# Four scores together, and VectorE's bias on the last two heads, in two attention stages of a transformer on one Trainium2 core

## The reference, cut to what matters

```python
# first attention (L0_attn)
scores = jnp.einsum('bhqd,bhkd->bhqk', q * scale, k)
scores = scores + position_bias * 8.0      # bucket of the distance, constant beyond 64
attn = jax.nn.softmax(scores, axis=-1)
ctx_out = jnp.einsum('bhqk,bhkd->bhqd', attn, v)
# rotary attention (in L2_ffn)
q = q * cos + _rotate_half(q) * sin
k = k * cos + _rotate_half(k) * sin
attn = jax.nn.softmax(jnp.einsum('bhqd,bhkd->bhqk', q, k) / sqrt(HD), axis=-1)
ao = jnp.einsum('bhqk,bhkd->bhqd', attn, v)
```

## Time and profile before

| | |
|---|---|
| time, median of 3 runs | 5949.95 us (5943.79 to 5955.69) |
| time of the profiled execution | 5956.9 us |
| its span | 5955.1 us |
| mean granted TensorE clock | 0.949 |
| busy: PE, PEld, DVE, ACT, POOL | 93%, 47%, 68%, 46%, 18% |
| first attention, first to last score | 81 to 969 us |
| rotary attention, first to last score | 2597 to 3348 us |

### The profile page before, as it was taken

How to read it: one execution, slowest core, us unless ns; L and a number is a source line. 1 busy time by engine, 2 the same in 40 slices (tenths; PEclk the granted TensorE clock), 3 DMA queues, 4 the chain that set the end, 5 groups by cost and what they waited for, 6 DMA issues and landing times. The chain is left out here.

```text
span 5955.1 us, 87145 instructions
## 1 busy us (share of the span) xinstructions
PE 5515.6 (93%) x32386; PEld 2785.2 (47%) x32386; DVE 4035.8 (68%) x7079; ACT 2747.2 (46%) x4392; POOL 1089.8 (18%) x731
## 2 busy tenths in 40 slices
PE   6999997789999999999999899979999999997999
PEld 2333333445477777742222377633333433434676
DVE  7888885775677777779989422367777777773412
ACT  4656665222233333357777534334444344442333
POOL 0110100220022232310120000023433333341000
PEclk7999998788999999999999899989999999998999
DMA  4211210001211111111111100000000000001000
GB/s 87 45 31 29 40 20 11 0 0 33 41 29 27 27 32 21 36 21 32 36 36 25 30 1 1 1 23 14 13 12 12 12 12 12 12 15 36 4 4 8
DMA packets 119335, 131.32 MB, mean 22 GB/s; under 512 B 44772, under 2 KB 68116, under 8 KB 118596
## 3 DMA queue, kind: packets, MB, share of 16 engines
q1 hardware_dynamic: 118408, 125.07, 10.1%
q10 hardware_dynamic: 504, 0.69, 0.1%
HBM read 102.29 MB, written 22.07 MB: 21 GB/s over the span
## 5 line engine op out<-in xcount | busy, mean ns | idle before, releaser
L3540 DVE TENSOR_REDUCE wide_max_parts<-wide_p 128x2 f32<-128x1024 f32 x512 | 613.8, 1219 | 133.2 <-PE wide_p L3444 120.8
L732 ACT ACTIVATE attn_w<-l_p 128x512 f32<-128x512 f32 x1024 | 549.3, 597 | 276.1 <-DVE l_p L1176 152.0
L2488 PE MATMUL caus_p<-caus_x_one,big 128*128 128x129 f32 x4608 | 639.8, 286 | 0.0
L583 DVE TENSOR_REDUCE l_max_parts<-l_p 128x2 f32<-128x1024 f32 x512 | 601.8, 1218 | 47.5 <-PE l_p L559 43.1
L2572 ACT ACTIVATE big<-caus_p 128x512 f32<-128x512 f32 (+3 forms) x768 | 345.5, 489 | 573.2 <-PE caus_p L2474 417.7
L583 DVE TENSOR_REDUCE rot_max_parts<-rot_p 128x2 f32<-128x1024 f32 x488 | 574.0, 1218 | 49.8 <-PE rot_p L559 47.5
L2488 PEld LDWEIGHTS caus_p<-caus_x_one,big 128*128 128x128 f32 x4608 | 590.2, 198 | 35.6 <-issue 2.2
L2932 ACT ACTIVATE moe_hidden<-moe_experts,moe_b 128x512 f32<-128x512 f32 x512 | 351.0, 687 | 527.0 <-PE moe_experts L2920 526.9
L3463 PE MATMUL wide_p<-wide_q,wide_k 64*128 64x512 f32 x2048 | 529.2, 595 | 0.0
L3643 ACT ACTIVATE attn_w<-wide_p 128x1024 f32<-128x1024 f32 x342 | 350.1, 1024 | 354.6 <-PE wide_p L3463 351.0
L2942 PEld LDWEIGHTS moe_experts<-big,moe_hidden 128*128 128x128 f32 x4096 | 474.2, 192 | 50.4 <-issue 49.3
(11 more groups left out here) (552 smaller groups left out, 8250.7 us busy)
## 6 DMA issues: line engine op xcount, KB each, us to landing
pair_q_stack<-q_parts SPq DMA_DIRECT2D x576, 32.0 KB
pair_k_stack<-k_parts SPq DMA_DIRECT2D x576, 32.0 KB
wide_inverse<-inverse_rows SPq DMA_DIRECT2D x64, 256.0 KB
l_q_stack<-q_parts SPq DMA_DIRECT2D x279, 32.0 KB
l_k_stack<-k_parts SPq DMA_DIRECT2D x279, 32.0 KB
big<-in_L_ffn_W SPq DMA_DIRECT2D x32, 256.0 KB, 5.9
q_parts<-pair_parts_q SPq DMA_DIRECT2D x8, 768.0 KB, 3.6
k_parts<-pair_parts_k SPq DMA_DIRECT2D x8, 768.0 KB, 3.6
```

The costliest lines, as they stand in the source:

```text
L583: self.nc.vector.tensor_reduce(self.max_parts[:, 2 * p:2 * p + 2, n, half], pair[:, :, 0:self.width(n, half)], AX.X, ALU.max).then_inc(*se ...
L732: self.nc.scalar.activation(self.exps[t % len(self.exps)], bank, ACT.Exp).then_inc(*self.exped.up())
L2488: mm = nc.tensor.matmul(outs[o % 2][:, nq % 2 * (C + 1):(nq % 2 + 1) * (C + 1)], exps[h % 2][:, kb, nq * P:(nq + 1) * P], x_one[b % 2][:, ...
L3540: nc.vector.tensor_reduce(max_parts[:, :, n, h], side, AX.X, ALU.max).then_inc(*maxed.up())
```

## The change

The four exps of a step now stand together, then the maxima, then the weigh. And VectorE's part of the near bias goes from heads 0 and 1 to heads 2 and 3 of the group, with the buffers, the loads and the indices turned accordingly. Numbers and shapes of all instructions and transfers stay.

```diff
-                out += exps[0:2] + maxima + exps[2:4] + weigh()
+                out += exps + maxima + weigh()
...
         if near is not None:
             bias, sem, n = near
-            first = bias.shape[2] - GROUP
...
-                                      bias[:, s, first + j, lo - kb * P:hi - kb * P], start=False,
+                                      bias[:, s, j, lo - kb * P:hi - kb * P], start=False,
...
-    ADDED = 2
+    ADDED, PARTED = 2, GROUP - 2
...
-                 if kind == "exp" and args[3] < ADDED and window(args[1], args[2])[0] < window(args[1], args[2])[1]]
+                 if kind == "exp" and args[3] >= PARTED and window(args[1], args[2])[0] < window(args[1], args[2])[1]]
...
                 for s in range(SPLITS):
                     nc.sync.dma_start(near_turned[:, s, :, :], near_window(
-                        core.near_parts[s], slice(first, first + ADDED))).then_inc(*near_loaded[g].up(16))
+                        core.near_parts[s], slice(first + PARTED, first + GROUP))).then_inc(
+                            *near_loaded[g].up(16))
                 for s in range(SPLITS):
-                    nc.sync.dma_start(near[:, s, rest * g:rest * (g + 1), :], near_window(
-                        core.near_parts[s], slice(first + ADDED, first + GROUP))).then_inc(
-                            *near_loaded[g].up(16))
+                    nc.sync.dma_start(near[:, s, PARTED * g:PARTED * (g + 1), :], near_window(
+                        core.near_parts[s], slice(first, first + PARTED))).then_inc(*near_loaded[g].up(16))
...
-                    weighted.exp_on_pe(pe, new, u, half, kb, j, bank, None if j < ADDED else (
-                        near[:, :, rest * g:rest * (g + 1), :], near_loaded[g], 32 * SPLITS))
+                    weighted.exp_on_pe(pe, new, u, half, kb, j, bank, None if j >= PARTED else (
+                        near[:, :, PARTED * g:PARTED * (g + 1), :], near_loaded[g], 32 * SPLITS))
...
-                    nc.vector.tensor_tensor(to, to, near_added[:, g, j, lo:hi],
+                    nc.vector.tensor_tensor(to, to, near_added[:, g, j - PARTED, lo:hi],
                                             ALU.add).then_inc(*added.up())
```

More of the change, by code:

```diff
@@ L1056, in load_near @@
                     sp.wait_ge(*near_made.at(g))
-                first, rest = GROUP * g, GROUP - ADDED
+                first = GROUP * g
                 for s in range(SPLITS):
                     nc.sync.dma_start(near_turned[:, s, :, :], near_window(
-                        core.near_parts[s], slice(first, first + ADDED))).then_inc(*near_loaded[g].up(16))
+                        core.near_parts[s], slice(first + PARTED, first + GROUP))).then_inc(
+                            *near_loaded[g].up(16))
                 for s in range(SPLITS):
-                    nc.sync.dma_start(near[:, s, rest * g:rest * (g + 1), :], near_window(
-                        core.near_parts[s], slice(first + ADDED, first + GROUP))).then_inc(
-                            *near_loaded[g].up(16))
+                    nc.sync.dma_start(near[:, s, PARTED * g:PARTED * (g + 1), :], near_window(
+                        core.near_parts[s], slice(first, first + PARTED))).then_inc(*near_loaded[g].up(16))
             load_near_max(0)
@@ L1118, in _ @@
                     u, half, kb, j = args
-                    rest = GROUP - ADDED
-                    weighted.exp_on_pe(pe, new, u, half, kb, j, bank, None if j < ADDED else (
-                        near[:, :, rest * g:rest * (g + 1), :], near_loaded[g], 32 * SPLITS))
+                    weighted.exp_on_pe(pe, new, u, half, kb, j, bank, None if j >= PARTED else (
+                        near[:, :, PARTED * g:PARTED * (g + 1), :], near_loaded[g], 32 * SPLITS))
                 elif kind == "near_turn":
```

## The result

The changed kernel takes 6132.82 us (median of 4 runs, 6127.23 to 6134.97), against 5950.55 us: a ratio of 1.0302, 95% interval 1.029 to 1.0315. Its profiled execution has a span of 6130.9 us, 175.8 us more than before, at a granted clock of 0.951 (0.949 before). From the first to the last score the first attention takes 954.8 us instead of 887.2, rotary 863.2 instead of 750.6: 67.6 + 112.6 = 180 us, so the whole loss lies in the two stages.

What follows compares the result with a forecast made beforehand. TensorE's queue was taken to bound both attentions. Rotary 132 us plus first attention 97, less 20 hidden and a few more, gave 205 us: 6155 us, 3.4% more, range 6065 to 6220.

Steps and rivals of the forecast that it cites:

- TensorE's queue paces both stages, and exp 3's wait for its bank sets the new step: Both attentions: TensorE is busy throughout quiet units; exp 3 would start 1.08 us behind exp 0, uncovered by maxima.
- plain rotary step: Rotary step without send, quotient or keep: 2.96 against 2.63 us, +0.33 in 244 steps with maxima, 81 us.
- Send, quotient, keep: Rotary's extra waits of exp 2 or 3: sends 29 us, quotients 16, keeps 6; first attention together 28.
- The first attention: Its steps: +0.41 us without window, +0.17 at 192 columns; with sends, quotients and keeps 97 us in all.
- What is hidden: At a batch's end, where VectorE leads, a longer TensorE queue costs nothing: 9 to 10 us per attention, -20 us.
- adjacency pays: Rival, both attentions: exp 3 does not wait, rotary gains 24 us and windowed steps some 10: 5915 us; 2%.
- Only exp 3's wait: Rival: sends, quotients and keeps cost nothing more because VectorE gets ahead of its reductions: 126 us more, 6076; 15%.
- VectorE hides half: Rival: VectorE hides far more, if half of the 205 us the time would be 6050; 6%.
- nothing changes: Rival: time the same within 0.2%, the waits vanishing behind something unseen; 1%.
- A falling clock: Rival: idling lowers TensorE's clock in both attentions; a tenth of them at 1.2 GHz would make 6320 us; 4%.

Runs made afterwards that it cites:

- the order alone: The kernel before with the new order of steps in both attentions, VectorE's bias still on heads 0 and 1: 6244.66 us, ratio 1.0495.
- five single banks: The changed kernel with five single banks and one pair for the maxima in both attentions, instead of three and two: 7066.96 us, measured once.

## Why the prediction was right

The forecast was 6155 us, the result 6133, in the range of 6065 to 6220: slower by 3.0% where 3.4% was forecast. Its steps, one by one:

**TensorE's queue paces both stages, and exp 3's wait for its bank sets the new step.** Shown: exp 3 at 1.08 in the changed kernel, at 0.66 with five single banks, a step of 2.72 with shorter exponentials, and no gain from those in the order before. The forecast of the plain rotary step was 2.96 and it is 2.93: the maxima cost 0.53 to the weigh, not 0.56 (244 x 0.03 = 7 us).

**Send, quotient, keep.** The mechanism is as described, with the releaser in the rows. Exp 2 of a send comes at 1.69 and not at 1.86, and the step is 3.77 - 2.93 = 0.84 us longer than a plain one; it was 0.06 before (2.69 - 2.63), so 0.78 where I had 0.9 (32 x 0.12 = 4 us). The size was to be had from the earlier trace rows: I put the end of the reductions at 0.70, from a plain step, but there the casts begin 2902.82 - 2902.30 = 0.52 behind exp 0. The same shift gives 0.52 + 0.86 - 0.33 = 1.05, where they begin now (3062.37 - 3061.32), and 1.05 + 0.58 + 0.05 = 1.68. Quotient 3.38 - 2.93 = 0.45 where I had 0.53, keep 0.19 as forecast.

**The first attention.** No window 3.20 (forecast 3.19), 192 columns 3.45 (3.44), a quiet unit 6.1 us longer (6.4). That the second half of the diff works for the change is shown by the order alone, 112 us slower than both.

**What is hidden: mis-sized.** In the prediction's sum this was the step with the largest error. I took 9 to 10 us for each stage, from TensorE's own waits for reductions. The two units of the first attention at a batch's end took 58.7 + 68.8 us before and take 62.1 + 71.3: 5.9 us more, where two quiet ones cost 12.3. Three batches hide some 20 us, and the last unit, with its short windowed steps (2.65 instead of 3.05), loses 1.1 instead of 6. The waits that show it are these, of the changed kernel:

```profile
PE l_p L559 <- DVE l_max_parts L583: 9.3, 13, 1.7
```

They were 22.5 in 28 waits. I had counted waits and not steps: VectorE's backlog also sits in the weight loads ahead of them (79.5 us in 138 waits before, 15.1 in 19 now), which suggests that more steps had something to give back. In rotary my 10 us were about right: fifteen units at 7.9 us more and the last at 2.5 would make 121, and the stage got 112.6 longer. So nearly all misses lie on one side: I had 132 - 10 = 122 us for rotary, where 112.6 came, and 97 - 10 = 87 for the first attention, where 67.6 came. The mechanism was right and the sum of 205 some 23 us too high.

**The rivals.** That adjacency pays is not borne out: with one change of shape less, the step is 0.30 longer. Only exp 3's wait (6076) is refuted by the rows of the sends. That VectorE hides half, or that nothing changes, is out: 182 of the 205 us came. A falling clock did not come in the changed kernel (0.98 and 0.99, as before), but came in the run with five single banks. The Trainium skill (TensorE: Matmul & The Clock Gate, A second HAM failure mode) describes a kernel that cycles through PSUM banks and whose clock swings between its two levels, because of many small idle times; here 0.42 us of them in every step did not lower the clock, and it fell in the run with waits of 1.3 us.

**Open.** Eight other arrangements of order, heads and banks were run and none beats the kernel before. One with VectorE's bias on three heads, which would use its slack of some 5 us a unit, was not tried.

## What to carry to other kernels

With n banks in a ring, the entry n places on waits for the first one's whole latency (product, read, release), so what does not use the ring should stand between the uses, long enough to cover it. Look for stretches where the kernel already runs in the other order, such as a tail: they price the change better than a sum of durations. And when two engines share one list, moving an entry moves it in both queues: price it on the engine that does it last, too.

## What the runs showed of the hardware

TensorE's granted clock held at 0.98 to 1.00 with an idle time of 0.4 us in each 2.9 us step, and fell to 0.77 and 0.81 of full speed, hence to the 1.2 GHz level for part of the time, in the run where a reduction stopped the queue for 1.3 us in each step of 4 us or more. That is one execution on one core. The 16 rotary steps of a unit had medians of 4.1 to 5.4 us in that run, where the waits alone make 4.0 in a plain one. A sum of durations at the full clock leaves this out. That the idle time is the cause is likely, since the clock fell in the two stages with it alone, but no run tests it by itself, and how much of the 7067 us it makes was not separated.
